# ScalarE's order of copy and square in the variance tiles, and the slot wait of their row loads

## The reference

```python
x1 = einsum('bct,bcd->bdt', x, L0_cond_weights[ids])      # 64x64 per sample
...
var = jnp.var(h, axis=-1)
log_var = jnp.log1p(var)
norm_var = log_var / (jnp.mean(log_var) + 1e-06)          # a mean over all rows
```

## Time and profile before

| what | value |
|---|---|
| median of 3 runs | 1458.44 us (1456.96 to 1459.35) |
| profiled execution, its own time | 1454.16 us |
| its span, first to last instruction | 1452.1 us |
| TensorE matmul busy | 1409.7 us, 97% of the span |
| DVE, ScalarE, GpSimd busy | 987.3, 874.8, 715.2 us |
| square of the variance tiles, line 247 | 64 times, 67.5 us |
| `v_lo`, line 256 | 64 times, 157.5 us |
| last variance tile's `v_lo` | about 268 us after the start |

### The profile page before, as it was taken

One profiled execution on the slowest core, in us unless ns is written; L12 is line 12 of the kernel. 1 busy time (PEld: TensorE's weight loads), 2 busy tenths in 40 slices (PEclk: granted clock), 3 DMA queues, 4 the chain that ended last, 5 costly groups with the idle time before them and its releaser, 6 DMA issues.

```text
span 1452.1 us, 28754 instructions
## 1 busy us (share of the span) xinstructions
PE 1409.7 (97%) x7300; PEld 895.1 (62%) x7300; DVE 987.3 (68%) x2745; ACT 874.8 (60%) x1842; POOL 715.2 (49%) x539
## 2 busy tenths in 40 slices
PE   6899999988999999999999999999999999999998
PEld 3677777654566666666666666666666666666665
DVE  5866888888666666666666666666666666666664
ACT  4667666565665666666666565565666555665662
POOL 4765666575544444444444444444444444444440
PEclk9999999988999999999999999999999999999999
DMA  9688556230333333333333333333333333333322
GB/s 310 214 297 271 187 183 203 95 106 17 101 98 98 110 100 102 102 107 96 99 96 96 100 100 111 97 96 96 96 96 96 105 104 98 97 96 97 113 87 80
DMA packets 160951, 176.14 MB, mean 121 GB/s; under 512 B 104851, under 2 KB 123238, under 8 KB 160785
## 3 DMA queue, kind: packets, MB, share of 16 engines
q1 hardware_dynamic: 156118, 161.56, 36.1%
q10 hardware_dynamic: 4795, 14.15, 2.9%
HBM read 135.97 MB, written 39.32 MB: 121 GB/s over the span
## 4 chain that ended last, share of the span: by engine, by line
PE 80%; POOL 8%; issue 5%; DVE 5%; ACT 1%; DMA 1%; POOLq 0%; SPq 0%; ACTq 0%; DVEq 0%
PE pair L86 21%; PE pair L87 20%; PE pair L88 20%; POOL v_lo L256 7%; PE pair L1717 6%; PE pair L1706 6%; PE pair L1536 1%; PE pair L1578 1%; PE pair L1577 1%; PE pair L1584 1%; DVE m_lo L1779 1%; PE pair L472 1%; DMA fourier<-in_fourier 1%; POOL m L1392 1%; POOL x_lo L1406 0%
## 5 line engine op out<-in xcount | busy, mean ns | idle before, releaser
L1404 POOL TENSOR_TENSOR t_narrow<-t_a_raw,t_narrow 128x256 f16<-128x256 f32 x64 | 52.0, 812 | 509.2 <-ACT x_hi L1205 509.2
L256 POOL TENSOR_TENSOR v_lo<-v_x,v_hi 128x1024 fp32r<-128x1024 f32 x64 | 157.5, 2466 | 88.2 <-ACT v_hi L250 88.1
L86 PE MATMUL pair<-m_hi,s_hi 128*128 128x512 f16 x512 | 196.1, 383 | 1.6 <-DVE c L1985 1.2
L87 PE MATMUL pair<-m_lo,s_hi 128*128 128x512 f16 x512 | 195.0, 381 | 0.0
L88 PE MATMUL pair<-m_hi,s_lo 128*128 128x512 f16 x512 | 194.9, 381 | 0.0
L1427 POOL TENSOR_TENSOR s_lo<-t_xt,s_hi 128x512 f16<-128x512 f32 x128 | 152.0, 1220 | 55.0 <-ACT s_hi L1211 55.0
L86 PE MATMUL pair<-t_narrow,x_hi 128*128 128x352 f16 x512 | 161.3, 315 | 2.2 <-POOL x_lo L1406 1.5
L87 PE MATMUL pair<-t_narrow,x_hi 128*128 128x352 f16 x512 | 160.6, 314 | 0.0
L88 PE MATMUL pair<-t_narrow,x_lo 128*128 128x352 f16 x512 | 160.6, 314 | 0.0
L1406 POOL TENSOR_TENSOR x_lo<-t_xt,x_hi 128x512 f16<-128x512 f32 x128 | 155.4, 1234 | 0.0
L86 PE MATMUL pair<-m_hi,x_hi 128*128 128x512 f16 x384 | 147.4, 384 | 0.0
(11 more groups left out here) (295 smaller groups left out, 3722.9 us busy)
## 6 DMA issues: line engine op xcount, KB each, us to landing
v_x<-in_x SPq DMA_DIRECT2D x64, 512.0 KB, 3.4
t_xt<-in_x_t SPq DMA_DIRECT2D x64, 512.0 KB, 3.2
out<-t_out_sb SPq DMA_DIRECT2D x64, 512.0 KB, 2.7
rhs_b<-bk_hi SPq DMA_DIRECT2D x256, 64.0 KB, 2.3
t_a_raw<-in_lora_a SPq DMA_DIRECT2D x128, 64.0 KB, 2.8
t_bd<-w_kinds SPq DMA_DIRECT2D x128, 64.0 KB, 2.2
t_rhs_c<-bk_lo SPq DMA_DIRECT2D x128, 64.0 KB, 2.3
blk_raw<-in_left_blocks ACTq DMA_DIRECT2D x10, 512.0 KB, 4.6
```

Source lines behind the costliest of these rows:

```text
L86: pe.matmul(out, a_hi, b_hi, start=start, stop=False, skip_group_check=skip)
L87: pe.matmul(out, a_hi, b_lo, start=False, stop=False, skip_group_check=skip)
L256: pool.tensor_tensor(v["v_lo"][:, s, :], v["v_x"][:, slot, :], f(v["v_hi"][:, s, :]), ALU.subtract).then_inc(v["v_lo_ready"], 1)
```

## The change

In `var_hi` the copy `v_hi` comes first, behind the waits for the rows and for the matmuls of tile n - 2; the square comes after it, behind a wait that keeps two squares of the same buffer apart. Since a slot of `v_x` is now last read by a square that comes after the copy, `var_load` waits until `v_lo` of tile n - 4 is done and not of tile n - 5: ScalarE's order then makes sure that the square of tile n - 5 is done. The wait for the weight slot stays. SP and GpSimd also wait for the last evacuation of ScalarE before the main stage.

```diff
@@ var_load
     used = sp.snap(n - (VSLOTS - 1)) if not isinstance(n, int) else n - (VSLOTS - 1)
+    squared = sp.snap(n - (VSLOTS - 2)) if not isinstance(n, int) else n - (VSLOTS - 2)
...
     if known_positive(used):
-        sp.wait_ge(v["v_lo_ready"], used)
+        sp.wait_ge(v["v_lo_ready"], squared)
     sp.dma_start(v["v_x"][:, slot, :], bass.AP(t["x"].tensor, x_off, [[HID, P], [1, HID]])
                  ).then_inc(v["x_loaded"][slot], 16)
@@ var_hi
     act.wait_ge(v["x_loaded"][slot], turn * 16)
     if known_positive(n - 1):
-        act.wait_ge(v["v_hi_ready"], n - 1)
-    act.activation(v["squares"][:, s, :], v["v_x"][:, slot, :], ACT.Square, accum_out=g["x_sq"][:, bass.ds(n, 1)])
-    if known_positive(n - 1):
         act.wait_ge(v["v_mm_done"], n - 1)
     act.copy(v["v_hi"][:, s, :], v["v_x"][:, slot, :]).then_inc(v["v_hi_ready"], 1)
+    if known_positive(n - 1):
+        act.wait_ge(v["v_hi_ready"], n)
+    act.activation(v["squares"][:, s, :], v["v_x"][:, slot, :], ACT.Square, accum_out=g["x_sq"][:, bass.ds(n, 1)])
@@ main_stage, sync
         sp.wait_ge(f_["c_chain"], 2 * KC + 1)
+        sp.wait_ge(f_["evac_hi_ready"], LBLK + KC)
@@ main_stage, gpsimd
         pool.wait_ge(f_["c_chain"], 2 * KC + 1)
+        pool.wait_ge(f_["evac_hi_ready"], LBLK + KC)
```

## The result

Six executions of the changed kernel took 1452.08 us at the median (1450.16 to 1453.98), six of the kernel before 1458.33 (1456.00 to 1460.97): a ratio of 0.9959, 95% interval 0.9948 to 0.9969, so 6 us faster. The forecast was 1454.2.

A forecast was written before the change was run, and what follows sets the result against it. TensorE was taken as the bound, only its gaps for `v_lo` winnable: 9.5 us of stall gains, cut by the supply of `x` to 4.2, so 1458.44 - 4.2 = 1454.2 us, range 1450.0 to 1459.5.

The forecast's parts named there:

- forecast without limit: First stage: the stall gains summed before any limit from the loads of `x`, 0.7 + 1.06 + 3.2 + 4.6 - 0.1 = 9.5 us.
- the caps: First stage: landing of `x` limits TensorE's lead, near 3 us at tile 23, 3.9 to 4.9 later; 4.2 us taken.
- Copy ahead of square, early tiles: Setup: 0.7 us from stalls at tiles 4, 7, 8; 1.06 at tile 9; 0.1 lost at `cs_hi`.
- Five stalls between 87 and 134 us: TensorE's waits for `v_lo` in this stretch, all under the 1.06 cap, would be gained whole: 3.2 us.
- Six q = 0 stalls: First tiles of blocks, tiles 29 to 54: stalls of 5.0 us, of which the cap leaves about 4.6 as gain.
- the DVE case: Rival, looped blocks: GpSimd's `v_lo` loses to DVE's `const_part`, q = 0 stalls stay; gain 2.5 to 3.5 us; 15%.
- The drift of SP: `var_load` in the loop: the second register value costs 0.07 us a tile, 3.5 us over 50 tiles.
- The first rival: Loads of `x` set no limit, the added register operation being fused away: gain 7 to 9.5 us, 1449 to 1451; 13%.
- The slot wait: `var_load`: waiting for a `v_lo` one tile later costs nothing by itself, since `v_lo` moves up with TensorE.
- The waits at the stage's end: SP's and GpSimd's new waits for the last evacuation cost nothing; it is done 2 us before.
- Main stage unchanged: After the first stage everything moves up whole; no change booked from 300 to 360 us, a us or two of scatter.
- what was to be seen: Signs: `v_lo` waits down to 3 or 4 us, second ALU row, five loads 18.5 us apart, some copies waiting for `v_x`.

The follow-up runs named there:

- the second profile: The changed kernel, not edited further, timed and profiled again beside the kernel before: 1452.05 us, ratio 0.9964.
- a dose in the loop: Changed kernel with one more id read by SP in each looped tile's load, ahead of the slot wait: 1478.24 us, ratio 1.0141.
- the kernels above: Changed kernel with tile 9's copy earlier (1453.59 us), `const_part` later (1449.04), both plus later id reads (1451.32), or `const_part` later and weight loads spread (1452.05).

## Why the prediction came out right, step by step

The direction and the mechanism of the gain were right: the copy comes sooner where ScalarE's queue held it. The size (4.2 forecast, 4.1 in the stage, 5.1 and 6.2 in medians) came out by luck. The forecast took 9.5 us and let the drift of SP's loads take 5.3 off. That drift hardly exists. In its place the gain was held down by three things: the five middle stalls gave nothing net (3.2 us less), the six q = 0 stalls gave 2.0 less with the small new stall at tile 30, the early ones 0.5 less, with 0.2 at `cs_hi` the other way. By stretches, each from the first matmul on:

| up to | gain | gain by then, forecast without limit |
|---|---|---|
| tile 10 | 1.5 us | 1.7 |
| tile 30 | 2.8 | 5.9 (limit put at about 3) |
| tile 45 | 4.4 | 8.2 |
| tile 63 | 4.1 | 9.5 (4.2 after the caps) |

- **Copy ahead of square, early tiles: right.** Tile 9's stall fell from 3.13 to 2.07 us, the square's 1.06. The stalls of tiles 4, 7 and 8 gave 0.24 (2.32 to 2.08), not 0.7; `cs_hi` came 0.14 sooner (12.65 us after the first matmul, before 12.79) where a loss of 0.1 was booked, and in the second profile 0.73 sooner, so this is chance.
- **Five stalls between 87 and 134 us, 3.2 us: wrong as a gain.** In their place stand five others (tiles 17 to 27) with 3.25 us. At tiles 23, 25 and 27 (2.7 us) the copies, a microsecond ahead, meet rows that haven't landed; at 17 and 22 (0.5 us) the rows were there and the copy stood behind ScalarE's own work, `blk_hi` last. That rows would limit this stretch was the right reason, with the place (tile 23) right and the size not: the cap was put near 3, and nothing was left. Tile 23's rows landed 4.3 us after issue, not 7.8, but SP issued them at 110.98 instead of 109.18, because one issue of a weight load took 1.30 us for 0.60 and a read of an id 2.02 us for 0.27 amid the burst; the copy waited 2.68 us for them. SP's reads of ids, by line:

```profile
L228 SPq TENSOR_LOAD <-cond_ids x118: 261/273/2022, 40.5 to 255.1; - x118
```

ScalarE's timeline at tile 23:

```profile
115.26 1.05 ACT L248 CAST v_hi<-v_x 128x1024 fp32r<-128x1024 f32 x1 [2.68 <-DMA v_x<-in_x]
```

- **Six q = 0 stalls, 4.6 us: a good half.** They fell from 5.0 to 2.2 us, 2.6 net of 0.2 at tile 30, and 1.4 of that is tile 29's alone, more than its cap of 1.06. The prediction gave the DVE case as all or nothing and 15%; it happened tile by tile, through the port (tiles 49 and 54, where `v_lo` takes 3.4 us for 2.4) and through DVE's gapless run up to `blk_lo` (tile 44). With `const_part` one tile later the six have 0.13 us left of 5.0.
- **The drift of SP, 3.5 us over 50 tiles, cap 3.9 at tile 52: wrong by five times in its price.** At 0.014 us a tile it is 0.7 us. The working took the row's 33 ns twice, for spacing; what was measured lies below both of its bounds (33 and 155 ns). Tile 52's rows were issued at 217.97 and landed 3.2 us later, its first matmul was at 226.97: by the prediction's 3.6 us from landing to matmul 2.2 us of lead were left, so the cap wasn't reached. The first rival's reason (no limit from SP) was true; its 7 to 9.5 us came only once DVE was out of the way (8.0 in that stage, of which 2.0 by tile 4, and 8.5 in the medians).
- **The slot wait costs nothing by itself: right in the new order,** and in the kernel with the waits alone the gap at tile 48 shows as later loads, not as lost time.
- **The waits at the stage's end cost nothing: not contradicted.** The main stage's first load leaves at 270.73, 2.8 us after the last variance tile's first matmul, as in the earlier trace rows (275.73 after 272.94).
- **Main stage unchanged, a us or two of scatter: right in kind;** the profiled pair differs by 2.45 us, a little more.
- Of what was to be seen: the stall waits fell to 6.1, not 3 or 4; five loads are 18.3, not 18.5 apart; no second ALU row appeared on SP (the one line has 30 operations, as before); copies wait for `v_x` in 21 of 64 tiles. In most tiles this would have been the sign of SP as the bound, so a third of them showed it without its cost.

## What to carry to other kernels

When a producer is moved up by taking work from ahead of it, list what bounds it next at each place: here rows in flight in one stretch, where five stalls of 3.2 us gave nothing net, and another engine on the port in the other, where half was kept. Here a short operation that started within 0.12 us of its rival for the port was worth a move by one tile (3.0 us). And price an added register operation by doing it: a dose in the loop (0.55 us a tile, 28 us) told at once how little lead there was, and the profile's five-tile distance how little the change had used of it.

## What the runs showed that was not expected

- A read of an id by SP took 0.27 us in the usual case and 2.02 us once, while four transfers of 512 KB were in flight; in the changed kernel a load of the rows landed 3.3 us after issue at the median from 140 to 215 us (3.1 to 4.0), and in the kernels above 7.1 to 8.9 us after it beside such transfers.
- A meeting of DVE and GpSimd costs both: 3.37 us of `const_part` against 1.27, and 8.26 us for three `v_lo` of 2.40 each. Their busy time rose by 3.5 and 5.5 us in the stage for the same instructions, so a busy share says little of their work.
- One pause of TensorE of 4.2 us, with full clock before it, was followed by a granted clock of 0.50 up to 120 us and 0.53 up to 122 us, and then by full clock again: eight matmuls started 0.36 to 0.59 us apart instead of 0.23, 1.7 us lost beside the pause itself.
